# Four convolution layers on one core: TensorE's three convolution loops written out, its operands read where they lie

## What is computed

```python
    x = x + _L0_conv_ref(_gn(x), L0_conv_weight, L0_conv_bias_p, L0_conv_gamma, L0_conv_beta)
    x = x + _L1_conv_ref(_gn(x), L1_conv_weights)
    x = x + _L2_conv_ref(_gn(x), L2_conv_weight, L2_conv_bias_p, L2_conv_gamma, L2_conv_beta)
    x = x + _L3_conv_ref(_gn(x), L3_conv_weight, L3_conv_idx_a, L3_conv_idx_b)
```

```python
        wb = binarize(weight)[0]
        out = jnp.einsum('bchwk,ochwk->bohw', patches, wb)
```

## Time and profile before

| | us |
|---|---|
| median of 3 runs | 824.02 |
| lowest, highest | 819.5, 826.45 |
| the profiled execution, time | 824.08 |
| its span in the trace | 822.1 |
| convolution stage of layer 0, first to last matmul | 55.3 to 153.4 |
| of layer 1 | 209.2 to 330.0 |
| of layer 2 | 354.4 to 453.5 |
| last stage | 526 to 822 |

### The profile page before, as it was taken

One profiled execution on the slowest core, in us unless ns is written; L12 is line 12 of the kernel. 1 busy time (PEld: TensorE's weight loads), 2 busy tenths in 40 slices (PEclk: granted clock), 3 DMA queues, 4 the chain that ended last, 5 costly groups with the idle time before them and its releaser, 6 DMA issues.

```text
span 822.1 us, 57420 instructions
## 1 busy us (share of the span) xinstructions
PE 541.4 (66%) x26570; PEld 407.4 (50%) x26570; DVE 588.2 (72%) x698; ACT 448.3 (55%) x724; POOL 294.9 (36%) x412
## 2 busy tenths in 40 slices
PE   0036556335799989346566166268998889989877
PEld 0025556234688878146555022145665556555554
DVE  4989999899542523699999896247676766767764
ACT  4229999490111211369998551136665655656653
POOL 1049884000655510088871040331414314132110
PEclk9996998758899999759989579569999988989997
DMA  8809999300499999249999000348889798887980
GB/s 340 365 12 357 395 397 397 156 1 0 158 341 354 399 400 411 111 145 395 395 398 365 17 1 0 83 147 318 289 321 362 252 380 297 308 314 255 401 320 23
DMA packets 49205, 213.36 MB, mean 260 GB/s; under 512 B 8960, under 2 KB 19200, under 8 KB 28672
## 3 DMA queue, kind: packets, MB, share of 16 engines
q1 hardware_dynamic: 39696, 205.87, 66.4%
q10 hardware_dynamic: 9216, 6.30, 2.5%
q0 software_dynamic: 240, 0.53, 0.2%
HBM read 193.79 MB, written 4.19 MB: 241 GB/s over the span
## 4 chain that ended last, share of the span: by engine, by line
PE 39%; DVE 21%; DMA 12%; POOL 10%; issue 8%; ACT 4%; SPq 3%; ACTq 1%; DVEq 0%; POOLq 0%
PE psum L828 12%; PE psum L938 10%; PE psum L911 8%; DVE stats L623 5%; POOL xn_ring L253 5%; PE psum L922 5%; DMA wring<-in_own 4%; DMA wring<-in_w 3%; DMA beyond<-state_b 2%; SPq L317 2%; POOL near L377 2%; DVE xn_ring L253 2%; ACT signs L466 2%; PE psum L838 2%; POOL state_a L366 2%
## 5 line engine op out<-in xcount | busy, mean ns | idle before, releaser
L791 DVE TENSOR_TENSOR state_b<-psum,state_b 128x512 f32<-128x512 f32 x256 | 175.2, 691 | 105.6 <-ACT state_b L590 99.3
L590 ACT ACTIVATE state_b<-psum 128x512 f32<-128x512 f32 x256 | 152.0, 597 | 115.3 <-PE psum L911 103.2
L828 PE MATMUL psum<-signs,near 64*32 64x96 f16 (+3 forms) x6528 | 124.3, 217 | 101.8 <-DMA beyond<-nothing 33.9
L828 PEld LDWEIGHTS psum<-signs,near 64*32 64x32 f16 (+1 forms) x6528 | 111.7, 103 | 110.6 <-issue 110.4
L691 DVE TENSOR_REDUCE abs_sums<-wring 128x1 f32<-128x2048 f32 x64 | 142.9, 2276 | 0.1
L911 PE MATMUL psum<-signs,sel 64*128 64x512 f16 x512 | 108.0, 419 | 46.2 <-POOL signs L400 21.6
L466 ACT ACTIVATE signs<-wring 128x2304 f16<-128x2304 f32 x64 | 135.1, 2111 | 0.0
L938 PEld LDWEIGHTS psum<-state_b,wring 128*32 128x32 f32 x8192 | 96.7, 117 | 76.1 <-issue 37.8
L938 PE MATMUL psum<-state_b,wring 128*32 128x32 f32 x8192 | 125.7, 205 | 12.0 <-DVE state_b L791 7.8
L828 PE MATMUL psum<-wring,near 64*32 64x96 f32 (+5 forms) x3264 | 95.9, 240 | 17.1 <-DMA beyond<-nothing 10.6
L828 PEld LDWEIGHTS psum<-wring,near 64*32 64x32 f32 (+1 forms) x3264 | 86.4, 108 | 24.2 <-issue 24.2
(11 more groups left out here) (141 smaller groups left out, 799.7 us busy)
## 6 DMA issues: line engine op xcount, KB each, us to landing
wring<-in_w SPq DMA_DIRECT2D x96, 1152.0 KB, 11.2
wring<-in_pairs SPq DMA_DIRECT2D x64, 1024.0 KB, 6.8
wring<-in_own SPq DMA_DIRECT2D x32, 256.0 KB, 6.4
wring<-signs SPq DMA_DIRECT2D x128, 64.0 KB, 2.0
state_a<-in_x SPq DMA_DIRECT2D x8, 512.0 KB, 9.7
out<-state_a SPq DMA_DIRECT2D x32, 128.0 KB, 6.8
beyond<-state_b ACTq DMA_DIRECT2D x112, 32.0 KB, 5.9
beyond<-state_a ACTq DMA_DIRECT2D x56, 32.0 KB, 5.9
```

Source lines behind the costliest of these rows:

```text
L590: act.activation(left[:, n % LSLOTS, :], psum[:, n % ASLOTS, :], ACT.Copy, scale=1.0 / HALF_SCALE / HALF_SCALE).then_inc(left_made, 1)
L791: dve.tensor_tensor(feats[:, n % FSLOTS, :], psum[:, ASLOTS + n % BSLOTS, :], left[:, n % LSLOTS, :], ALU.mult).then_inc(feats_made, 1)
L828: last = pe.matmul(psum[g * B:(g + 1) * B, bank, (a * C) % 512:(a * C) % 512 + (b - a) * C], acts[q, j, s, k, :], weights[q, j, kind, s, ( ...
```

## The change

PE's convolution stages are no longer loops: `conv` takes the block number `m` as a Python number and is written out 32 times per layer. With that each piece can have addresses of its own, and PE reads the normalised pieces where they lie in the other state tensor: `here` is piece j of block m, `above` of block m+1, `below` of block m-1. The matmuls that would multiply zeros at the edges are left out. Gone are `near`, `beyond`, `nothing`, POOL's `copy_near`, ACT's `load_beyond`, and the computed counts; PE waits for constants, and takes over the wait for the normalised pieces (`wait_normed(pe, layer, needed(n))`). The loop of the last stage stays; it gets `head_slot`, which fixes the place of its first instruction in PE's code. All else, the order of the matmuls too, is as it was.

```diff
-        near = sb("near", [P, PIECES, PIECE], F32)[:, :, :]
-        beyond = sb("beyond", [P, PIECES, PIECE], F32)[:, :, :]
-        nothing = sb("nothing", [P, PIECE], F32)[:, :]
...
-            def copy_near(layer, n):
-
-                m, j = divmod(n, PIECES)
-                wait_normed(pool, layer, order(m, j))
-                if n >= PIECES:
-                    pool.wait_ge(conv_done, CHUNKS * layer + n - PIECES + 1)
-                dst, src = near[:, j, :], normed(layer, m, j)
-                if layer != 1:
-                    dst, src = dst.bitcast(F16), src.bitcast(F16)
-                pool.tensor_copy(dst, src).then_inc(near_made, 1)
...
-                    copy_near(layer, n)
...
-            def load_beyond(layer, n):
-
-                m, j = divmod(n, PIECES)
-                wait_normed(act, layer, needed(n))
-                for quad, other in ((0, m + 1), (G - 1, m - 1)):
-                    q = slice(quad * C, (quad + 1) * C)
-                    src = normed(layer, other, j)[q, :] if 0 <= other < BLOCKS else nothing[q, :]
-                    act.dma_start(beyond[q, j, :], src).then_inc(beyond_in[j], 16)
...
-                        load_beyond(1, n)
...
-                    load_beyond(layer, n)
...
-            def conv(layer, it, j, started):
-
+            def conv(layer, m, j, started):
+
+                n = PIECES * m + j
                 binary = layer != 1
-                pe.wait_ge(near_made, it * PIECES + (CHUNKS * layer + j + 1))
-                pe.wait_ge(beyond_in[j], it * 32 + (32 * BLOCKS * layer + 32))
+                wait_normed(pe, layer, needed(n))
                 if j < 2:
-                    pe.wait_ge(bank_free[j], it + (BLOCKS * layer + 1))
+                    pe.wait_ge(bank_free[j], BLOCKS * layer + m + 1)
                 if binary:
-                    pe.wait_ge(signs_made, it * PIECES + (CHUNKS * (layer // 2) + j + 1))
...
+                    pe.wait_ge(signs_made, CHUNKS * (layer // 2) + n + 1)
                 else:
-                    pe.wait_ge(w_in[j], it * 16 + 16 * loads(1, j))
-                    pe.wait_ge(rest_made, it * PIECES + (j + 1))
...
+                    pe.wait_ge(w_in[j], 16 * loads(1, n))
+                    pe.wait_ge(rest_made, n + 1)
...
+                def acts(block):
+
+                    if not 0 <= block < BLOCKS:
+                        return None
+                    t = normed(layer, block, j)
+                    if binary:
+                        return t.bitcast(F16).rearrange("p (k s b) -> p s k b", k=2, b=B)
+                    return t.rearrange("p (s k b) -> p s k b", k=1, b=B)
+
+                here, above, below = acts(m), acts(m + 1), acts(m - 1)
                 pairs = [(2, 0, 2, here), (0, 0, 2, here), (1, 2, 2, here), (2, 2, 2, here)]
-                singles = [(0, 3, 1, there), (0, 2, 1, here), (1, 1, 1, here), (1, 0, 1, there)]
+                singles = [(0, 3, 1, below), (0, 2, 1, here), (1, 1, 1, here), (1, 0, 1, above)]
...
+                                    if src is None:
+                                        continue
...
-                with pe.Fori(0, BLOCKS) as it:
+                for m in range(BLOCKS):
                     started = set()
                     for j in range(PIECES):
-                        conv(layer, it, j, started)
+                        conv(layer, m, j, started)
...
-            with pe.Fori(0, NGROUP - 1) as j:
+            with nc.Fori(0, NGROUP - 1, engines=bass.OrderedEngineSet([pe.engine]), head_slot={pe.engine: 0}) as j:
```

More of the change, by code:

```diff
@@ L134, in build @@
         mats_in = sem("mats_in")
-        nothing_set = sem("nothing_set")
         sel_made = sem("sel_made")
@@ L141, in build @@
         conv_done = sem("conv_done")
-        piece_begun = sem("piece_begun")
         bank_free = sems("bank_free", 2)
-        near_made = sem("near_made")
-        beyond_in = sems("beyond_in", PIECES)
         rest_made = sem("rest_made")
@@ L349, in _ @@
                 pool.dma_start(dst, src).then_inc(consts_in, 16)
-            pool.memset(nothing, 0.0).then_inc(nothing_set, 1)
             centre = [0]
@@ L501, in square_row @@
                 act.activation(sq_row[:, e % 2, :], rows_of(state_b, e), ACT.Square).then_inc(row_squared, 1)
-            act.wait_ge(nothing_set, 1)
             for layer in range(3):
@@ L805, in conv @@
                 if binary:
-                    pe.wait_ge(signs_made, it * PIECES + (CHUNKS * (layer // 2) + j + 1))
-                    weights, here, there = signs, near.bitcast(F16), beyond.bitcast(F16)
-                    here, there = (t.rearrange("p j (k s b) -> p j s k b", k=2, b=B) for t in (here, there))
-                else:
-                    pe.wait_ge(w_in[j], it * 16 + 16 * loads(1, j))
-                    pe.wait_ge(rest_made, it * PIECES + (j + 1))
-                    weights, here, there = wring, near, beyond
-                    here, there = (t.rearrange("p j (s k b) -> p j s k b", k=1, b=B) for t in (here, there))
@@ L814, in conv @@
-                pe.sem_inc(piece_begun, 1)
-                weights = weights.rearrange("p n (l s r) -> p n l s r", l=KINDS, s=COLS)
+                    pe.wait_ge(signs_made, CHUNKS * (layer // 2) + n + 1)
+                else:
+                    pe.wait_ge(w_in[j], 16 * loads(1, n))
+                    pe.wait_ge(rest_made, n + 1)
+                weights = (signs if binary else wring).rearrange("p n (l s r) -> p n l s r", l=KINDS, s=COLS)
+                def acts(block):
[5 more added lines that the diff above has]
+                    return t.rearrange("p (s k b) -> p s k b", k=1, b=B)
@@ L825, in conv @@
                                 bank = a // (W // 2)
-                                for g, (kind, quad, count, acts) in enumerate(tiles):
+                                for g, (kind, quad, count, src) in enumerate(tiles):
+                                    if src is None:
+                                        continue
                                     q = slice(quad * C, (quad + count) * C)
                                     last = pe.matmul(psum[g * B:(g + 1) * B, bank, (a * C) % 512:(a * C) % 512 + (b - a) * C],
-                                                     acts[q, j, s, k, :],
+                                                     src[q, s, k, :],
                                                      weights[q, j, kind, s, (a - col + 1) * C:(b - col + 1) * C],
```

## The result

The changed kernel takes 977.09 us (median of 4 runs, 968.99 to 982.01) against 822.67 us (median of 4, 819.5 to 826.45): a ratio of 1.186 with an interval of 1.180 to 1.192, slower by 154.4 us. The profiled span went from 822.1 to 974.5 us. Forecast were 950 us and a range of 880 to 1040.

A forecast was written before the change was run, and what follows sets the result against it. After the change PE was taken to be bound by fetching its own code in all three layers: 44.5 + 43.4 + 37.7 = 125.6 us on the profiled 824.08, giving 950 us, range 880 to 1040.

The forecast's parts named there:

- The kind of stall: All three convolution layers: PE bound by its own code, with "issue" stalls every 126 records, 30 or more in each.
- 31.6 fetches: Layers 0 and 2, after the signs of piece 2: (4216 - 238)/126 fetches, at 4.3 us 135.9 us.
- The waits that PE took over: Convolution stages: three waits hold nothing back, as the normalisation runs four or more pieces ahead.
- The two paces of present code: Code already present runs 126 records in 2.9 us in layer 1 and 2.8 us in layers 0 and 2.
- The size of a fetch: All three layers: 4.3 us for each fetch of 126 records; 3.6 to 5.2 us gave the range.
- four samples: Kernel before, PE short of code: 4.14, 3.95, 6.47 and 3.47 us from one resumption to the next.
- Load on the fetch: Convolution layers: fetch time goes with DMA load; a share of 60 to 68% expected, a little above the first two samples.
- the first rival: Convolution layers: short fetches, the turnaround stays at 3.47 us; +42, 866 us; chance 0.11.
- The copies: 96 POOL copies and 192 ACT DMA issues removed: costed at zero; 1.7 us per binary layer if PE's code kept up.
- the second rival: Convolution layers: fetches hidden in straight code, 9 us faster, 815 us; chance 0.07.
- The last stage: Same loop with its head at a fixed slot: zero, at most one fetch more or less, 4 us; unchanged at 296 us.
- The slower clock: PE may get its lower clock level more often; in layer 1 126 records up to 5.8 us; kept in the upper end.

The follow-up runs named there:

- the weights thinned: The changed kernel with every weight chunk behind the first eight loading only 288 of 2304 columns: 894.22 us (2 runs).
- the kernel with half the code: The changed kernel without the low half's matmuls in layers 0 and 2 (2108 of 4216 records left in each): 873.07 us, ratio 1.062.

## Why the prediction held

**The kind of stall.** Right. 118 packets were forecast and 118 came, 31 stalls with "issue" in layer 0 for 31.6 fetches, and DVE and ACT wait for PE. The DMA share is 0.58 to 0.65, forecast 0.60 to 0.68. That written-out code alone brings the loss, and that the time follows the amount of code, the experiments show. The waits that PE took over held back little, as forecast: PE idled 1.3 us for POOL's halves in layer 2. The two paces of present code that the forecast compared its samples with were read loosely: the piece of 3.49 us has 160 records and not 152, which makes 2.75 us per 126, and the 2.8 us of layers 0 and 2 are the pace of DVE and ACT, not of TensorE's code. Both are below every sample, so nothing hung on it.

**The size of a fetch.** This is the term that was mis-sized. 4.3 us was taken, between the median and the mean of four samples. From ACT's signs of piece 2 in layer 0 (done 60.31) to the last matmul (204.67) are 144.4 us for 31.6 fetches, 4.57 us each. In layer 1 177.2 us for 37.5 are 4.73. In layer 2 the signs of piece 2 are done at 463.41 + 2.11 = 465.52, and 146.9 us for 31.6 are 4.65. The mean of the four samples, 4.51, was nearer than their median: where stalls add up it is the mean that counts, and the long ones of 6 us (layer 2's chain above) are part of it. With four samples from 3.47 to 6.47 us that the true mean fell inside the range of 3.6 to 5.2 was likely, not certain. That the step could be told from the mean DMA share was wrong as well: 0.6 was taken to give a little over 4 us, and the steps of 5.9 to 6.4 us in layer 2 stand at 0.57. How the sum came out:

| | forecast | measured |
|---|---|---|
| layer 0 | +44.5 | 204.67 - 153.42 = +51.3 |
| layer 1 | +37.7 | 436.12 - 329.97 less 51.3 = +54.9 |
| layer 2 | +43.4 | 612.4 - 453.5 less 106.2 = +52.7 |
| behind it | 0 | 362.1 - 368.6 = -6.5 |
| sum, on the span | +125.6 | +152.4 |

Layer 0: 0.27 us x 31.6 = 8.5 more, less 1.7 us because the signs of piece 2 came earlier (60.31 for 62.0): 6.8, which is the difference. Layer 1: 0.43 x 37.5 = 16.1, and it began only 1.6 us sooner behind layer 0 (258.94 - 204.67 = 54.3 for 55.8) where 2.8 were forecast: 17.3 for 17.2. Layer 2: 0.35 x 31.6 = 11.1, less 1.7 us because it began sooner behind layer 1 (465.52 - 436.12 = 29.4 for 361.03 - 329.97 = 31.1): 9.4 for 9.3.

**Load on the fetch.** That the fetch lengthens with the DMA engines' load was right in sign (3.9 us with the weights thinned, 4.7 in the changed kernel, some 6 beside the full weight stream of the kernel with half the code), but with hardly any load a fetch is not as short as the shortest sample: 3.8 to 4.0 us on average. The changed kernel has the first rival's 3.47 us only in stretches such as the end of layer 0.

**The copies.** Costed at nothing once PE is last. Without the written-out code they are worth 12 us (expected by the second rival for its case: 9), and in written-out code the kernel without them was 34 us faster. So "zero" was too simple. The 408 records fewer are 3 fetches, some 15 us, and the forecast did count these. Between the two profiles lie 39.4 us: 28.6 of them up to the end of layer 2, and 10.8 in the last stage, which the copies don't touch. What makes up the rest of the 28.6 is not settled; the distance of fetches is nearly the same with the copies (4.63 in layer 0) and without.

**The last stage.** Forecast unchanged; 6.5 us shorter. In the profiles in which no pass fetches again its matmuls spread over 282 to 294 us, with and without the slot, against 290 before, so this is in the spread of profiles and luck for the sum.

**The slower clock.** Kept in the upper end, and it came: 0.53 in the binary layers. It cost nothing measurable there, since even a slow run, 2.6 to 3.0 us, ends before the next code is there; in layer 1 it is part of the 4.73 us, by an amount that no run separates.

**The rule.** The second rival was the Trainium skill's, page "Runtime: NRT & Kernel Launch", section "Instruction fetch mechanics": the next block is fetched during the current one and mostly hidden. In the changed kernel it is not hidden, at runs of 2.6 to 3.0 us a block, and with half the code it isn't either (32.6 us of stalls in layer 0); it only costs no time there, since DVE and ACT take 98 us for 16.7 fetches anyway. Only the part of a fetch that lies beneath the run of the block in hand is hidden. Code written out was the dearer form here, by 19% without the copies and 23% with them.

## What to carry over

Divide the time that a stage takes for other reasons by its number of fetches, one for 126 matmuls with their loads. At 2.8 to 3.1 us a fetch (the three layers before) straight code set the pace instead, at 3.3 to 6.4 us a fetch, and a loop whose body stays present was faster; at some 6 us a fetch (half the code) it cost next to nothing. Between these nothing was measured, and how long a fetch takes depends on the load of the DMA engines. Such a bound shows in no busy share but in packets on the instruction queue and in "issue" stalls, one for each fetch, and the first passes through the loops of the kernel before gave its price in advance within 10%. Reading in place and writing out are two edits, worth -12 us (with the loops) and +189 us (with the copies) by themselves and +154 together, so they don't simply add. The first can be had without the second only where the addresses can be computed in the loop, and that was not tried.

## What was not expected of the hardware

- A loop body of 8.6 blocks (two blocks of the picture) is fetched anew in each pass, while those of layers 0 to 2 (4.3 and 4.8) are fetched once. The Trainium skill, page "Runtime: NRT & Kernel Launch", section "Instruction fetch mechanics", gives TensorE's instruction memory as 2048 instructions, eight such blocks; both bodies agree with it. The last loop at slot 200 does not fit so simply, as the next point shows.
- The last stage takes 12 packets in all or 49, by where the head of its loop lies (as before, or at slot 200): four of fifteen passes fetch 9 packets and take some 35 us for 16.6. Why four, and which, is open.
- A fetch stays long on nearly idle DMA engines: with their share at 0.14 to 0.21 it still took 3.8 to 4.0 us on average, and 3.30 to 3.45 in its shorter steps, though its packet carries 16 KB.
- A 32 KB transfer took 2.1 us (median, end of layer 0) with no chunks queued and 6.4 us behind 1152 KB chunks.
- A granted clock of 0.50 to 0.53 (the lower of its two levels, 1.2 GHz) cost the binary stages nothing. Nor does its row tell the speed of the matmuls: in the kernel with half the code TensorE was busy half of the time in layers 0 and 2 alike, the row had 1.00 in the one and 0.50 in the other, and the matmuls of 96 columns took 273 to 274 ns in both, for 217 to 223 in layer 0 of the kernel before, where the row had 0.88.
